# Reordering the hand-over from projections to attention in a fused float32 transformer layer

## What is computed

```
q = x @ wq   (16 heads of 16)      k, v = x @ wk, x @ wv   (4 heads of 16)
q, k = rotary(q), rotary(k)
attn = softmax(q k^T / 4) v        (4 query heads share a k/v head)
x = layernorm(x + attn @ wo)
g, u = x @ Wg^T, x @ Wu^T          (Wg, Wu, Wd dequantized from int32, 1024 wide)
x = layernorm(x + (silu(g) * u) @ Wd^T)
```

## Time and profile before

| what | value |
|---|---|
| time, median of 3 runs | 904.97 us (902.16 to 907.14) |
| the profiled execution: time | 901.66 us |
| the profiled execution: span of the core | 899.8 us |
| mean granted TensorE clock | 0.992 |
| PE busy | 98% of the span |
| DVE busy | 83% |
| ACT busy | 79% |
| POOL busy | 30% |

### The profile page before, as it was taken

The page is one execution under the profiler, slowest core; times in us unless marked ns, Lnnn a source line. Parts: engine busy times, 40 slices in busy tenths (PEclk is TensorE's granted clock), DMA queues, the critical chain, the costliest instruction groups (busy, mean ns, idle before and its releaser), DMA issues.

```text
span 899.8 us, 16217 instructions
## 1 busy us (share of the span) xinstructions
PE 880.8 (98%) x5658; PEld 459.5 (51%) x5658; DVE 742.7 (83%) x1655; ACT 713.4 (79%) x929; POOL 268.5 (30%) x232
## 2 busy tenths in 40 slices
PE   8999999999999999999999999999999999999996
PEld 3334444444444444444444444444436888888885
DVE  5578999999999999999999999999955455665545
ACT  1467999999999999999999999999985565555564
POOL 6763340035434000001001000220104765665555
PEclk9997999999999999999999999999999999999999
DMA  7993543323353132232214313131111010110001
GB/s 245 292 242 97 122 123 85 88 84 76 93 120 70 45 77 58 56 77 68 52 48 91 73 46 78 44 62 36 39 54 52 30 48 24 48 47 25 24 24 48
DMA packets 53458, 69.98 MB, mean 78 GB/s; under 512 B 17344, under 2 KB 26560, under 8 KB 53376
## 3 DMA queue, kind: packets, MB, share of 16 engines
q1 hardware_dynamic: 50280, 65.53, 28.8%
q0 software_dynamic: 864, 3.15, 1.3%
q10 hardware_dynamic: 2232, 0.25, 0.2%
HBM read 46.74 MB, written 16.25 MB: 70 GB/s over the span
## 4 chain that ended last, share of the span: by engine, by line
PE 84%; DVE 5%; DMA 3%; ACT 2%; issue 2%; POOL 1%; SPq 1%; ACTq 0%; POOLq 0%; DVEq 0%
PE pv_bank L1367 25%; PE ring_bank L1279 23%; PE pair_bank L1425 13%; PE pair_bank L1488 12%; PE pv_bank L1514 3%; PE ring_bank L1514 3%; DVE block_max L846 3%; PE ring_bank L1377 2%; DMA q_sb<-shift 1%; ACT probs L1180 1%; PE pair_bank L1313 1%; DMA q_parts<-low 1%; DMA sinq_sb<-sin_q 1%; POOL rotated L588 1%; PE ring_bank L1392 1%
## 5 line engine op out<-in xcount | busy, mean ns | idle before, releaser
L1180 ACT ACTIVATE probs<-pair_bank 128x1024 f32<-128x1024 f32 x512 | 495.8, 1023 | 43.6 <-PE pair_bank L1425 43.4
L846 DVE TENSOR_REDUCE block_max<-ring_bank 128x1 f32<-128x384 f32 x854 | 486.2, 608 | 16.9 <-PE ring_bank L1279 7.2
L1279 PE MATMUL ring_bank<-k_max,q_sb 48*128 48x512 f32 x1126 | 313.4, 443 | 1.8 <-DVE block_max L842 0.5
L1279 PEld LDWEIGHTS ring_bank<-k_max,q_sb 48*128 48x128 f32 x1126 | 151.1, 185 | 267.0 <-DVE block_max L846 116.5
L1367 PE MATMUL pv_bank<-probs,v_all 128*17 128x512 f32 x2048 | 270.5, 600 | 0.7 <-ACT probs L1180 0.7
L1425 PE MATMUL pair_bank<-q_sb,k_sb 50*128 50x512 f32 x1024 | 221.8, 428 | 2.5 <-DMA q_sb<-shift 1.7
L1037 DVE SCALAR_TENSOR_TENSOR hid<-pair_bank,up_s,silu 128x512 f32<-128x512 f32 x63 | 47.1, 747 | 85.1 <-ACT silu L1236 85.1
L1425 PEld LDWEIGHTS pair_bank<-q_sb,k_sb 50*128 50x128 f32 x1024 | 99.4, 186 | 30.7 <-ACT probs L1180 9.2
L755 POOL TENSOR_TENSOR hid_l<-hid,hid_h 128x512 fp32r<-128x512 f32 x63 | 81.7, 1297 | 86.3 <-ACT hid_h L1215 85.6
L670 POOL TENSOR_TENSOR attn<-attn,inv_rows 128x1024 f32<-128x1024 f32 x7 | 16.7, 2390 | 301.7 <-DMA inv_rows<-inv_d 228.6
L842 DVE CUSTOM_DVE_ANT_0 above<-ring_bank,above 128x512 f32<-128x512 f32 x136 | 93.2, 687 | 5.8 <-PE pair_bank L1279 3.9
(11 more groups left out here) (142 smaller groups left out, 862.9 us busy)
## 6 DMA issues: line engine op xcount, KB each, us to landing
k_max<-k_parts SPq DMA_DIRECT2D x96, 96.0 KB, 3.7
q_sb<-q_parts SPq DMA_DIRECT2D x64, 128.0 KB, 3.5
k_sb<-k_parts SPq DMA_DIRECT2D x96, 64.0 KB, 2.3
attn<-xT SPq DMA_DIRECT2D x8, 512.0 KB, 6.0
q_parts<-high SPq DMA_DIRECT2D x16, 256.0 KB, 3.7
q_parts<-low SPq DMA_DIRECT2D x16, 256.0 KB, 4.3
q_sb<-q_parts SPq DMA_DIRECT2D x64, 64.0 KB, 3.7
attn<-pv_sb SPq DMA_DIRECT2D x128, 32.0 KB
```

The source lines that it names most:

```text
L846: dve.reduce_max(block_max[half % 2][:, col:col + 1], bank[:, 0:width], axis=AX.X).then_inc(ring_used, 1)
L1180: act.activation(probs[t % 2][:, 2 * pr:2 * pr + 2, :], pair_bank[pr][:], ACT.Exp, scale=D ** -0.5).then_inc(probs_ready, 1)
L1279: pe.matmul(bank[:, 0:last - first], q_sb[k][rows, i, qt * P:(qt + 1) * P], k_max[k // QH][rows, kind * CH + first:kind * CH + last], star ...
```

## The change

Four edits, all around the hand-over. (1) POOL's `low_of(7, 0)` waits for the first `turn_shift`, and SP issues `load_shift(0, 0)` before `store_q(7, 0)`. (2) ACT's two copies `copy_v_rows(3)` and `copy_k_rows(3)` are made between entries of the last list, after its second and its sixth entry. (3) The last list goes round 5 banks in another order, and the bank that is left over is written by a filler matmul (`keep_busy`: 128 rows, 128 weight columns, 128 moving columns, float32, nobody reads the result) ahead of each entry but the first, 12 in all. (4) At g = 0 all five entries come ahead of both scores, each behind a filler, 5 in all.

```diff
+VALUES_COPIED = 1
+KEYS_COPIED = 5
+WIDE_BANKS = 5
@@ early_place
-            turn = (pos - wide_from) % (2 * BANKS)
-            return BANKS + turn if turn < BANKS else (wide_from + turn) % BANKS
+            turn = (pos - wide_from) % WIDE_BANKS
+            return (2 * BANKS - 1, BANKS)[turn] if turn < 2 else (wide_from + turn - 2) % BANKS
@@ SP, projections
+                    if last and c == 1:
+                        load_shift(0, 0)
                     store_q(m, 0)
...
-                    if last and c == 1:
-                        load_shift(0, 0)
                     store_q(m, 1)
@@ POOL
+            def after_turn(half):
+                pool.wait_ge(shift_ready, half + 1)
@@ POOL, low_of
+                if m == BLOCKS - 1 and j == 0:
+                    after_turn(0)
                 pool.wait_ge(hi_ready, 2 * m + j + 1)
@@ ACT, early_takes
-                for key in early[n, h]:
+                for at, key in enumerate(early[n, h]):
...
+                    if n == BLOCKS and at == VALUES_COPIED:
+                        copy_v_rows(B - 1)
+                    if n == BLOCKS and at == KEYS_COPIED:
+                        copy_k_rows(B - 1)
@@ ACT, before the last list
-            copy_k_rows(B - 1)
-            copy_v_rows(B - 1)
@@ PE
+            def keep_busy(bank):
+
+                pe.matmul(bank, wq_sb[:, 0, 0:P], x_in[BLOCKS - 1][:, 0, 0:P], start=True, stop=True)
+
             def early_work(n, h):
-                for key in early[n, h]:
+                for at, key in enumerate(early[n, h]):
+                    if n == BLOCKS and at:
+                        keep_busy(pair_bank[0][:, 1, 0:P])
@@ PE, attention, scores
-                                for index in ((BANKS, BANKS + 1), (BANKS + 2, BANKS - 1))[pr]:
+                                for index in ((BANKS,), (BANKS + 2, BANKS - 1))[pr]:
@@ PE, attention, step g
-                        if t in MIXED:
+                        if first and k == 0 and t == 0:
+                            for i in range(len(entries)):
+                                keep_busy(pv_bank[:, 0:P])
+                                maxima(i)
+                            scores(0)
+                            scores(1)
+                        elif t in MIXED:
```

More of the change, by code:

```diff
@@ L661, in _ @@
             pool.wait_ge(v_used, 2 * B)
-            def after_turn(half):
-                pool.wait_ge(shift_ready, half + 1)
             def normalize(p):
```

## The result

The changed kernel takes **916.75 us** (median of 6, 915.14 to 921.68) against 903.41 us for the kernel before (median of 6, 900.05 to 907.14): ratio 1.0155, 95% interval 1.0127 to 1.0183, slower by 1.3 to 1.8%. The prediction was 907.2 us, no change that can be told, in a range of 900.5 to 916. The prediction was wrong: a change clear of the noise came where none was forecast, the time lies just outside the range, and what happened is the rival "the clock falls all the same" (chance 0.24, 916 us). The profiled execution took 915.99 us with a span of 914.1.

A forecast was written before the change was run, and what follows sets the result against it. PE, busy 98% of the span, bounds the kernel; only the hand-over changes. Scores(0) 7.1 us later less 2.7 back through the clock, then +4.2 on 901.66, gave 905.9; allowing for the median, 907.2 us, range 900.5 to 916.

The forecast's parts named there:

- the clock falls all the same: Rival at the hand-over: clock falls near 70 us, before the entries are through; +14 us, 916 us (910 to 918); chance 0.24.
- Now the sum at the full clock: Hand-over: full-clock steps put scores(0) at 79.35, 7.1 us later, and the second pv at 85.0, +4.4 us.
- The price of a step: PE in the last list: one maxima entry with one filler takes 0.84 us at full clock, about 1.5 at half.
- the case of cheap fillers: Rival in the last list: fillers hide in waits, steps down to stream alone, 0.53 us; 899.4 to 905 us; chance 0.18.
- The rival's working: Hand-over with the clock fallen: scores(0) at 87, second pv at about 95, +14 us, 916 us; chance 0.24.
- The end of the sum: Behind the second pv PE is bound by its own work, so nothing changes there.
- The own case: Hand-over: fillers at 0.84 us a step and the clock kept; 907.2 us, range 904.5 to 909.5; chance 0.45.
- the third rival: Behind scores(0): clock falls while PE waits for two exponents, 2 to 4 us more, 908 to 911 us; chance 0.13.
- Edits 1 and 2 disappear behind PE: Last list: with fillers PE sets the pace and no reader is late, so these edits gain nothing.
- the 0.6 to 0.7 us of the prediction: Last list: earlier turn and copies alone end DVE's and ACT's work 0.6 to 0.7 us earlier, if PE keeps up.
- A smaller term: Median 904.97 lies 3.3 us above the profiled execution; whether to add that gave 906 or 909.2, and 907.2 was taken between.

The follow-up runs named there:

- version 7: Changed kernel with its fillers in the maxima's own form (48 rows, 512 columns, float32r) instead of 128 rows: 904.0 us, ratio 0.9997.
- version 5: Changed kernel with fillers of 256 moving columns instead of 128: 912.38 us, ratio 1.0102.
- version 6: Changed kernel with fillers of 512 moving columns instead of 128, the size of a projection matmul: 918.08 us, ratio 1.0148.
- version 2: Kernel before with only the first turn ahead of POOL's low parts and ACT's copies between entries: 901.66 us, ratio 0.9983.
- version 4: Changed kernel without the 12 fillers of the last list, the 5 of step 0 kept: 906.87 us, ratio 1.0028.
- version 8: Changed kernel without any filler and with the 6 banks of before, maxima still ahead of the scores: 903.86 us, ratio 0.9992.
- version 10: Changed kernel with 48-row fillers, seven more ahead of step 1's exponent waits, and one projection-sized filler near 37 us: 903.06 us, ratio 1.0007.
- version 3: Changed kernel without the 5 fillers of step 0, the 12 of the last list kept: 911.7 us, ratio 1.0092.
- version 11: Kernel before with edits 1 and 2 and one projection-sized filler at the load wait near 37 us: 901.77 us, ratio 0.9978.

## Why the prediction was wrong

**What failed** is one step, the condition of the sum: "Now the sum at the full clock". Weighing the two cases, the prediction gave 0.45 to the clock kept and 0.24 to its fall before the entries are through. It fell at about 71 us, in the list and as early as before, and was back at 95. All 6 executions have a mean clock of 0.977 to 0.983, where the kernel before has 0.984 to 0.992 in all but two of its executions beside the versions (0.982 and 0.983 there), so this is the rule and not a chance of one.

**The price of a step was right.** 0.84 us was worked out from the period of the projections, and 0.84 to 0.85 was measured; 1.45 us at half clock against "about 1.5". The rule of the Trainium skill that was weighed against it ("TensorE: Matmul & The Clock Gate", Step-by-step: what each phase is for), weight loads pulled ahead, would have made it 0.63 by the prediction's estimate. In this mix the trace shows none pulled ahead: the filler's load is at 66.50, 0.43 us behind the entry's at 66.07, and the next entry's at 66.91. Stream alone, 0.53, which the case of cheap fillers took as its bound, was far off for 128 rows, and even too high for 48 (version 7: 0.35 to 0.38).

**The rival's working was right too**: scores(0) at 87 (86.74), second pv at about 95 (95.25), 916 us (915.99 the profiled execution, 916.75 the median). That the places agree so closely is in part luck: the list began 1.1 us later than assumed, and from its first entry it was 20.7 us to scores(0) where the working had 22. The end of the sum, that nothing changes behind the second pv, held to 0.3 us.

**Why the clock fell.** What decided it was the columns of the fillers. With 128 it fell in the list; with 256, all else alike, it stayed through the same list (version 5), and with 512 too (version 6). Whether the switches have a part in it is not shown, since no version varies them alone. Putting the loss together: version 5 less the 17 x 0.21 us that its fillers stream more is 912.4 - 3.6 = 908.8 us, an estimate of the changed kernel with the clock kept through the list. So of the 13.3 us some 5.4 are what the change costs with the clock kept through the list (17 fillers of 0.42 us, 7.1, less what PE gets back), and 8 are clock. The own case, 907.2, is 1.6 us from the estimate; but version 5 still loses the clock behind scores(0), and so the estimate belongs rather to the third rival, "the clock falls later", 908 to 911.

**The weighing.** The prediction had its clue on the table: before the fall PE ran maxima with waits, and a step of 0.84 us "streams for only 0.43 us, half of it in 48 rows". It set against this that the projections never lost the clock. But they stream 1.07 us of 1.48 in the same pattern, and so were no evidence for a step of 0.43 in 0.84: their step is version 6's, not the change's. Nor do they always keep it: in the profiled executions of versions 2, 4 and 8 the clock was at half among the projections, for 3, 14 and 7 us from about 40 us on.

**A smaller term.** The 3.3 us between the median of three and the profiled execution, of which the prediction added 1.3, was a chance of three: with six executions the median of before is 903.41, 1.8 us above it.

**Edits 1, 2 and 4.** "Edits 1 and 2 disappear behind PE" fits the waits of ACT for PE above; no version has the fillers without these edits. Alone they give about 1.7 us (version 2, ratio 0.9983), more than the 0.6 to 0.7 us of the prediction, within an interval that holds both.

## What to carry to other kernels

A filler that keeps an engine's clock up has to be costed like any work in an in-order queue: price the step from a stretch with the same alternation, and count load and switches, not only columns. Small ones pay the full load and switch each time and may lose the clock as well: here 17 of 128 columns lost more than 17 of 256, and as much as 17 of 512 (916.75, 912.38 and 918.08 us). Before adding any, bound the prize: here the executions of version 10 with the clock held all the way were 2.2 to 3.6 us faster, less than the 5.4 us that 17 fillers cost even with the clock kept through the list.

## What the runs showed that was not expected

More work made the kernel faster: 17 x 128 more columns, 4.4 us less. The clock also fell at a second place in some executions, near 40 us, after PE had stood for the first maxima's data. Timeline of PE in version 2:

```profile
34.70 1.98 PE L1324 MATMUL pair_bank<-attn,wq_sb 128*128 128x512 f32 x4
38.55 0.47 PE L1286 MATMUL pair_bank<-k_max,q_sb 48*128 48x512 f32 x1 [1.87 <-DMA k_max<-k_parts]
...
38.97 2.04 PE L1324 MATMUL pair_bank<-attn,wq_sb 128*128 128x512 f32 x2
40.80 1.06 PE L1300 MATMUL ring_bank<-ident,v_rows 128*128 128x128 f32 x4
```

A projection matmul that takes 1.12 us at other places took 2.04 here, and the transposes 1.06 instead of 0.60. The wait ahead of it, for the data of the first maxima, was 0.69 us in the profiled execution of before and 1.87 here. Its length alone does not decide: in version 3 the clock stayed full behind 1.72 us, in version 4 it fell behind 1.59.

What makes one execution of a kernel slower than another can be read where the slowest was the profiled one. Windows of version 4 (914.10 us):

```profile
41.00:54.00 13.00, 12.79 (x25) 3.80 (x24) 4.34 (x11) 5.83 (x13) 6.26 (x5) 0.50 0.82 273
75.00:98.00 23.00, 22.30 (x77) 10.66 (x78) 11.91 (x28) 10.79 (x15) 7.17 (x7) 0.50 0.38 110
```

And of version 8 (909.50 us), which has no filler at all:

```profile
72.00:92.00 20.00, 18.61 (x70) 8.72 (x71) 12.55 (x29) 11.86 (x18) 7.38 (x7) 0.50 0.44 126
```

Both were at half clock at two places, near 40 us (14 and 7 us) and at the hand-over (24 and 20 us, where the kernel before had 10). So a fall of 20 us and more at the hand-over comes without fillers in the list too, in some executions; with the 17 fillers of the change it came in all. The spread of 900 to 908 us between executions of one kernel goes with the time at half clock. The wait near 40 us is not shown to be its source: version 2 fell there and took 900.93 us, and the filler that fills this wait stands in version 11, where no execution is over 902.7 us, and in version 10, where five of 12 are over 905.

What stays open is what sets how long the clock stays at half, and how the chip weighs rows, columns and gaps: 48-row fillers held the clock in some executions and not in others, at the same instructions.
